# Two last feed-forwards in one program: the ninth step's and the tenth step's work interleaved, with storage of its own for the tenth

## The reference

```
x = x + tanh(g_xattn[0]) * xattn(layernorm(x), ctx)        # 16 heads of 32
x = x + tanh(g_ffn[0])   * ffn(layernorm(x))

xattn: q = int8_linear(x, wq) + bq        # rows and weights rounded to 127 steps
       k = ctx @ wk.T + bk ; v = ctx @ wv.T + bv
       o = softmax(q k.T / sqrt(32) + mask) v
       return int8_linear(o, wo) + bo
ffn:   qx = fp8(x / row scale)                        # 512 columns
       g, u = qx @ w_gate.T, qx @ w_up.T              # 1408 columns each
       t = silu(g) * u ; qt = fp8(t / row scale)
       return qt @ w_down.T
```

## Time and profile before

| | |
|---|---|
| median of 3 runs | 636.78 us (636.06 to 639.3) |
| the profiled execution's own time | 635.0 us |
| its span, first to last instruction | 633.2 us |
| mean granted TensorE clock | 0.936 |
| VectorE busy | 544.7 us, 86% of the span |
| TensorE matmuls busy | 486.6 us, 77% |
| ScalarE busy | 476.3 us, 75% |
| GpSimd busy | 226.3 us, 36% |

### The profile page before, as it was taken

One profiled execution on the slowest core, in us unless ns is written; L12 is line 12 of the kernel. 1 busy time (PEld: TensorE's weight loads), 2 busy tenths in 40 slices (PEclk: granted clock), 3 DMA queues, 4 the chain that ended last, 5 costly groups with the idle time before them and its releaser, 6 DMA issues.

```text
span 633.2 us, 10703 instructions
## 1 busy us (share of the span) xinstructions
PE 486.6 (77%) x3200; PEld 309.3 (49%) x3200; DVE 544.7 (86%) x1354; ACT 476.3 (75%) x1160; POOL 226.3 (36%) x210
## 2 busy tenths in 40 slices
PE   1558487758998899899979988999899877582733
PEld 1546366436744665475446545754575453241311
DVE  2799898879899999999999899989999986876683
ACT  0697699989987799689878887988799876742150
POOL 1402422102362447154524452454337232702310
PEclk9889679989999999999999999999999996967768
DMA  8814543540133013202410250034004100000000
GB/s 284 267 40 126 159 122 95 136 125 14 27 90 104 33 41 97 83 34 61 119 39 35 67 149 34 4 80 137 35 5 97 34 35 1 1 1 34 0 1 33
DMA packets 52106, 45.54 MB, mean 72 GB/s; under 512 B 7889, under 2 KB 42705, under 8 KB 52049
## 3 DMA queue, kind: packets, MB, share of 16 engines
q1 hardware_dynamic: 45504, 31.48, 17.8%
q0 software_dynamic: 3488, 12.85, 6.4%
q10 hardware_dynamic: 3056, 0.54, 0.5%
HBM read 23.87 MB, written 4.19 MB: 44 GB/s over the span
## 4 chain that ended last, share of the span: by engine, by line
DVE 36%; PE 28%; issue 12%; ACT 10%; SPq 1%; DMA 1%; POOL 1%; DVEq 0%; ACTq 0%
DVE prob L1233 6%; DVE ts L1427 4%; PE bank_u L775 3%; DVE q L1134 3%; DVE gate L1293 3%; PE bank_t L819 3%; PE bank_g L775 3%; PE bank_s L756 2%; DVE t_sb L1181 2%; PE bank_a L762 2%; PE bank_o L859 2%; ACT prob L571 2%; PE bank_g L989 2%; DVE t_sb L1129 2%; PE bank_g L995 2%
## 5 line engine op out<-in xcount | busy, mean ns | idle before, releaser
L571 ACT ACTIVATE prob<-prob,neg_max 128x256 f32<-128x256 f32 x256 | 127.2, 502 | 4.3 <-DVE neg_max L1233 4.3
L1233 DVE CUSTOM_DVE_ANT_0 prob<-bank_s,mask_sb 128x256 f32<-128x256 f32 x256 | 97.0, 418 | 12.6 <-PE bank_t L819 6.8
L819 PE MATMUL bank_t<-ident,prob 128*128 128x128 f32 x512 | 79.9, 281 | 26.8 <-ACT prob L571 19.8
L368 POOL TENSOR_TENSOR up<-up,wgu_scale 128x512 f32<-128x512 f32 (+1 forms) x42 | 56.6, 1347 | 89.0 <-ACT up L551 89.0
L582 ACT ACTIVATE probT<-bank_t 128x512 f32<-128x512 f32 x128 | 74.5, 589 | 18.5 <-PE bank_t L819 18.0
L819 PEld LDWEIGHTS bank_t<-ident,prob 128*128 128x128 f32 x512 | 60.6, 143 | 48.9 <-ACT prob L571 33.5
L378 POOL TENSOR_TENSOR up<-gate,up 128x512 f32<-128x512 f32 (+1 forms) x48 | 64.4, 1341 | 23.2 <-DVE up L1297 17.5
L756 PE MATMUL bank_s<-kk,qq 128*128 128x256 f16 x256 | 48.1, 283 | 23.9 <-DVE neg_max L1233 12.6
L383 POOL TENSOR_TENSOR x<-x,qf 128x512 f32<-128x512 f32 x14 | 19.3, 1380 | 106.1 <-DVE qf L1441 106.1
L775 PE MATMUL bank_g<-wguT,x2T 128*128 128x512 bf16 (+1 forms) x192 | 47.8, 373 | 4.1 <-DVE gate L1293 3.3
L571 ACT ACTIVATION_READ_ACCUMULATOR prob<-prob,neg_max 128x1 f32 x256 | 49.8, 195 | 0.0
(11 more groups left out here) (204 smaller groups left out, 1202.0 us busy)
## 6 DMA issues: line engine op xcount, KB each, us to landing
qq<-rows SPq DMA_DIRECT2D x128, 64.0 KB, 2.0
x_in<-in_x_dram SPq DMA_DIRECT2D x8, 512.0 KB, 3.6
c_in<-in_ctx_dram SPq DMA_DIRECT2D x8, 512.0 KB, 3.6
kk<-hi SPq DMA_DIRECT2D x64, 64.0 KB
kk<-lo SPq DMA_DIRECT2D x64, 64.0 KB
out_dram<-x POOLq DMA_DIRECT2D x8, 512.0 KB, 3.2
t_sb<-in_L_ffn_w_down_dram POOLq DMA_DIRECT2D x4, 704.0 KB, 6.8
mask_sb<-in_mask_BxSxS_ff_dram SPq DMA_DIRECT2D x8, 256.0 KB, 3.8
```

The costliest lines, as they stand in the source:

```text
L368: pool.tensor_tensor(up[:, c % 2, 0:w], up[:, c % 2, 0:w], wu_scale[:, off:off + w], ALU.mult).then_inc(s["u_scaled"], 1)
L571: ins = act.activation(prob[:, head_par, t, :], prob[:, head_par, t, :], ACT.Exp, bias=neg_max[:, head_par, t:t + 1], scale=-1.0, accum_ou ...
L819: ins = pe.transpose(T_BANK[1 - hp][:, lc * N + t * P:lc * N + (t + 1) * P], prob[:, 1 - hp, t, lc * P:(lc + 1) * P], ident[:, :])
L1233: ins = dve.tensor_tensor_reduce(prob[:, hp, t, :], S_BANK[hp][:, t * L:(t + 1) * L], mask_sb[:, hb, t, :], -1.0, 3.4e38, ALU.add, ALU.min ...
```

## The change

Two things change together.

**The ninth and tenth steps become one program.** `step` becomes `blocks`, which returns the blocks of one step; the order is then written for one step or, in `tail_order(k, e)`, for two: `k` is step 8 (heads of batch 7, feed-forward of batch 6), `e` is step 9 (feed-forward of batch 7). The tenth step's blocks get a second set of names through one table, with dead buffers of the attention (`x_in`, `qq`, `kk`, `c_in`, `wkT`, `wvT`, `wqT`, `v_sb`), the two score banks in place of G and U, and semaphores of their own (`s_last`). New waits guard the reuse: `oqT_turn` for the last mask, the copies for the last q and v projection. Still shared are `rows`, `xq`, `y2` and the engines.

```
+        FFN = ((x2, gate, up, th, (t_sb[:, 0, :], t_sb[:, 1, :]), q8, mag, x2T, *turned_views(turned[:, :]), stats2, mv2, ve2, rstd2,
+                x2s, ts_, G_BANK, U_BANK),
+               (x_in, gate_up_last[:, 0], gate_up_last[:, 1], c_in[:, 1, :],
+                tuple(w[:, :, :].rearrange("p c o -> p (c o)")[:, 0:I] for w in (wkT, wvT)),
...
+                var2_last[:, 0, :], var2_last[:, 1, :], x2s_last, ts_last, S_BANK[0], S_BANK[1]))
...
+        s_last = {n: sem(n + "_last") for n in names[names.index("oqT_ps"):names.index("stored")]}
...
-            def step(b, par, A, NEW, OLD, D, W):
-                B2 = b - 2
+            def blocks(b, par, A, NEW, OLD, D, W):
+                d, f = (2, s_last) if b == NB + 1 else (b, s)
+                B2 = d - 2
...
                 def oqT_turn(slot):
                     pe.wait_ge(s["o_rounded"], b - 1)
-                    pe.wait_ge(s["y2_ready"], 1 + 2 * B2)
-                    pe.wait_ge(s["tT_out_act"], 1 + 2 * B2)
+                    if not OLD:
+                        pe.wait_ge(s["masked"], 16 * NB)
+                    pe.wait_ge(f["y2_ready"], 1 + 2 * B2)
+                    pe.wait_ge(f["tT_out_act"], 1 + 2 * B2)
...
-                    for t, bk_ in enumerate((A_BANK, O_BANK if W else U_BANK)):
-                        if t == 1 and D:
+                    for t, bk_ in enumerate((A_BANK, U_BANK if A and not W else O_BANK)):
+                        if t == 1 and A and D:
...
+            tail_order(blocks(NB, 0, False, False, True, True, False), blocks(NB + 1, 1, False, False, False, True, False))
```

**All other orders are written anew.** Steps 0, 1 and 2 to 7 have other lists on PE, DVE and ACT, and slightly other ones on POOL in steps 0 and 1. The same blocks are called. POOL no longer waits right behind `out_store`; `x2_add` waits for the store instead:

```
                 def x2_add(slot):
+                    need(pool, s["stored"], 16 * B2)
...
                     pool.dma_start(out[bass.ds(b - 2, 1)].rearrange("o (t p) c -> p (o t) c", p=P), x2[:, :, :]).then_inc(s["stored"], 16)
-                    pool.wait_ge(s["stored"], 16 * (b - 1))
...
-                    load(4); x_var(0); load(6); load(8); load(10); x_plus_bias(4); load(12); load(14)
+                k.load(4); k.x_var(0); k.x_plus_bias(4); k.load(6); k.load(8); k.load(10); k.load(12); k.load(14)
```

More of the change, by code:

```diff
@@ L1 @@
+from collections import namedtuple
 from contextlib import ExitStack
@@ L20 @@
 LEAD = 12
+PoolBlocks = namedtuple('PoolBlocks', """load x_var x2_add x2_var x_plus_bias up_scale gate_up out_add out_store""")
+ActBlocks = namedtuple('ActBlocks', """pro_v pro_round_o wo_scaled oqT_high k_high_1 xT_high tT_high up_copy t_mag_0 t_mag_1 t_mag_2 head_exp head_probT group_oT
+ctxT_copy o_round k_high_0 x_centre x_round x2_mag_0 x2_mag_1 q_high gate_tanh unit_copy unit_mag""")
+PeBlocks = namedtuple('PeBlocks', """pro_turn_v pro_turn_o wo_scale_turn head_score head_turn oqT_turn ctxT_turn group_pv x2T_turn o_turn sx_turn unit_turn
+k_project_even k_project_odd v_project_low v_project_high xT_turn q_project_0 first_score y_project gate_project up_project
+q_project_1 tT_turn down_project_low down_project_high""")
+DveBlocks = namedtuple('DveBlocks', """pro_v pro_int_o pro_o x_stats oqT_low head_mask xT_low x2T_copy sx_copy tT_low v_evac o_norm o_max o_scales gate_scale unit_round
+unit_scale q_low_0 t_mul y_scale x_scales x2_stats x2_centre x2_max k_low_0 bias_scale x2_sum_0 x2_sub_0 k_low_1 x2_sum_1 x2_sub_1
+t_sum_0 t_sum_1 t_sub_0 t_sub_1 t_sum_2 t_sub_2 t_mul_last q_scale_0 q_low_1 t_scales y2_scale""")
 def need(eng, sem, count):
@@ L1363, in x2_max @@
[L1363 to L1366 removed]
+                    dve.wait_ge(f["x2_centred"], d - 1)
+                    dve.tensor_reduce(x2s[:, 0, :], rows[:, :, :], AX.X, ALU.max, apply_absolute_value=True).then_inc(f["x2_scaled"], 1)
@@ L1491, in _ @@
-            step(0, 0, True, True, False, False, True)
-            step(1, 1, True, True, True, False, True)
+                        dve.wait_ge(f["y2_ready"], 1 + 2 * B2 + t + 1)
+                        dve.tensor_tensor(x2[:, t, :], x2[:, t, :], y2, ALU.add).then_inc(f["out_ready"], 1)
+                return DveBlocks(
+                    pro_v, pro_int_o, pro_o, x_stats, oqT_low, head_mask, xT_low, x2T_copy, sx_copy, tT_low, v_evac,
+                    o_norm, o_max, o_scales, gate_scale, unit_round, unit_scale, q_low_0, t_mul, y_scale, x_scales,
+                    x2_stats, x2_centre, x2_max, k_low_0, bias_scale, x2_sum_0, x2_sub_0, k_low_1, x2_sum_1, x2_sub_1,
+                    t_sum_0, t_sum_1, t_sub_0, t_sub_1, t_sum_2, t_sub_2, t_mul_last, q_scale_0, q_low_1, t_scales,
+                    y2_scale)
```

664 lines of the change are left out of this document (357 added, 307 removed).

## The result

The changed kernel is slower: a median of 648.9 us (647.4 to 650.4, 4 runs) against 636.5 us (636.1 to 639.3, 4 runs), ratio 1.018 with a 95% interval of 1.013 to 1.022. Forecast were 622 us and faster.

The account below looks back on a forecast made before the run. VectorE was taken to bound the steady steps, with 31.5 us idle in the tail. Starting 18.9 us earlier, less 3.9 pushed back, gave 15.0, taken as 14; other steps zero: 635.0 to 621.0, as a median 622 us, range 613 to 630.

Parts of the forecast that it names:

- The tail: Ninth and tenth steps: batch 7's row scales come 18.9 us earlier by overlapping; 14 us gained after imperfect gap filling.
- The "up to 2 us": TensorE's clock in the last two steps: fewer pauses could bring back up to 2 us more; none counted.
- The steady steps: Six steady steps in the new order: VectorE's work the same, zero change per step, bound 1 us either way.
- my walk: One steady step followed through the new order; after the six chunks it stood within 0.3 us of the trace.
- the POOL rival: Tail: POOL's `gate_up` and `out_add` collide with VectorE and hold back the overlap; 9 us gained, 627 us; chance 0.10.
- The slower rival: Steady steps: `k_high` comes no earlier, VectorE stalls 2.8 us at `k_low` in each of six, 639 us; chance 0.05.
- The stall ahead of `k_low`: Steady steps: VectorE waits for ScalarE's `k_high`, which ends near 403.9; 0.3 to 0.8 us of stall.
- Steps 0 and 1: First two steps: moving `x_plus_bias` earlier could give up to 2.9 us; taken as 0, with 3 us either way.
- POOL's store wait: Steady steps: POOL's wait for the landed store moves to `x2_add`, which comes after it anyway; costs nothing.

Follow-up runs that it names:

- e1: Changed kernel with steps 0, 1 and the steady steps back in their old orders, so only storage and merged tail are new: 621.0 us, 0.974 of the kernel before.
- e6: As e1, but in the steady steps all engines except VectorE have their new lists: 666.7 us, 1.048 of the kernel before.
- e10: Changed kernel with the second `q_low` moved one place ahead of `gate_scale(9)` in VectorE's steady list: 633.3 us, 0.993 of the kernel before.
- e12: As e1, but `v_evac(11)` put ahead of `t_sub_1(10)` in VectorE's old steady list: 621.9 us, 0.977 of the kernel before.
- e8: As e1, but GpSimd's two feed-forward products cut to 16 columns in the steady steps: 611.2 us, 0.959 of the kernel before.
- e7: Changed kernel with old orders in steps 0 and 1, and GpSimd's two feed-forward products cut to 16 columns in the steady steps: 618.0 us, 0.968 of the kernel before.
- e11: Changed kernel with `k_low_0` moved behind `x2_max` and `head_mask(4)` in VectorE's steady list: 650.4 us, 1.023 of the kernel before.
- e4: Changed kernel with all orders put back, last two steps one after the other; only new storage, semaphores and waits stay: 635.2 us, 0.995 of the kernel before.
- e2: Changed kernel with new orders in the steady steps only, old orders elsewhere, last two steps one after the other: 664.4 us, 1.043 of the kernel before.
- e3: Changed kernel with new orders in steps 0 and 1 only, old orders elsewhere: 638.9 us, 0.998 of the kernel before.
- e5: As e1, but in the steady steps VectorE alone has its new list: 711.9 us, 1.118 of the kernel before.

## Why the prediction was wrong

**The tail: right.** Forecast were a last mask 30.6 us behind the step's start, a last `group_pv` at 35.4, row scales at 41.1 and a last addition at 101; they came at 30.5, 35.8, 41.5 and 103.3, with `oqT_turn` 1.4 us behind the row scales. Of the 14 us forecast the changed kernel shows 12.0, and the new tail alone 14.2. What lies between goes with TensorE's clock (no run changed the clock by itself): with the same tail lists the tail takes 99.9 to 100.1 us in the four profiles where the two parts were granted 0.96 and 0.83 (e1, e6, e10, e12), and 100.9 to 103.3 us at 0.88 to 0.92 and 0.77 or 0.78 in the six others. The "up to 2 us" that I left uncounted was real, and went either way. Idle time in the two steps fell from 31.5 to 19.9 us, not to 17, and from the row scales to the last addition VectorE is busy 84%, just under the 85% forecast. Of the last batch's first tile `t_sum` did meet GpSimd (mean 1193 ns) and so did `t_mul` (901), but `t_sub` stays at 635 to 648, and as many collisions went as came: VectorE's busy time in the tail is 83.4 us, before it was 83.9.

**The steady steps: the step that failed.** "I take zero per step, with a bound of 1 us either way": it was 3.9 us a step, 23.3 in all. The walk behind it used undisturbed durations for operations that were given new neighbours. I had the collision in a row, 1.49 for 0.69, and the rule beside it, and applied both to the tail's GpSimd work alone; in the steady steps "VectorE's work is the same" passed for a reason. The work was the same and its times were not. That "my walk stood within 0.3 us of the trace" was no test of this, since the old order has only some 2 us of stretching in a step: VectorE is busy 9.9 us more over the six in e1 than in e8, and 12.6 more in the kernel before. What the new order showed in place of zero was 17 us of collisions and 6 us of waits over the six steps. One row was misread beside this: the 728 ns of `t_sub` in the earlier trace rows is a mean over 512 and 384 columns, whose undisturbed value is 642 to 644 (e7, e8), not 692, so the old tail had more than twice the stretching that the POOL rival was told of; the forecast does not hang on it.

**The slower rival** had the right place for a small wait and the wrong price for a loss. The stall ahead of `k_low` is 0.84 us a step, just above the 0.3 to 0.8 of the walk, and e11 shows that taking it away gains nothing there. The other waits (`gate_scale`, most of it for TensorE, 5.5 us against 0.9, and `oqT_low` for the transposes, 4.2 against 0.6) were not foreseen; with `k_low`'s 5.0 they outweigh what went elsewhere, and the 6.2 us between e7 and e8 is what they cost. Which of them carries how much was not tried.

**Steps 0 and 1** lie inside "0, with 3 us either way" by the means over profiles (2 us), though the one profile of the result shows 5.8. The collision of the earlier trace rows did go (VectorE is busy 116.4 us there instead of 118.9), and it bought no time. **POOL's store wait** costs nothing (e4). The end of the program became 1.6 us shorter in all kernels with the new storage and waits, e4 too; by what part of them is open.

Best of all kernels that do the whole work is e1: the change's storage and merged tail with the old lists everywhere else, 621.0 us, 2.6% under the kernel before and 4.3% under the changed one. The blind forecast of 622 us was in effect one for e1.

## What to carry to other kernels

When a list is reordered, an operation's duration belongs to its new neighbours, not to itself. For each VectorE operation with SBUF inputs alone, look whether it would start inside a GpSimd operation, and charge it with what is left of that; put operations that read a PSUM bank there instead (inside a product `gate_scale`, the masks and `v_evac` kept their 0.75, 0.42 and 0.68 us). A swap of one place made 12.6 us in six steps (e10), and another one none, since the next operation's end was set by GpSimd's next product (e12): walk on at least to the next gap of GpSimd. And a change that comes as several lists of orders is best measured list by list in time but with all engines together: the differences of e1, e2 and e3 to e4, added to e4's time, give 653.9 us where 648.9 was measured, but e5 and e6 were 65 and 20 us slower in six steps than the slower of the two full sets.
